# Second cross attention: value projections filled for four heads and two key tiles at a time, with three value buffers and half the DMA scratch of GpSimd

## The reference

```python
x = layernorm(x, gamma_media, beta_media)            # context, 1601 rows
latents = layernorm(latents, gamma_lat, beta_lat)    # the decoder's 512 rows
kv = concatenate((x, latents * kv_gate), axis=1)     # 2113 rows
q = (latents @ Wq).reshape(b, n, 8, 64)
k = (kv @ Wk).reshape(b, f + n, 8, 64)
v = (kv @ Wv).reshape(b, f + n, 8, 64)
sim = einsum('bqhd,bkhd->bhqk', q * SCALE, k)
sim = sim - max(sim, axis=-1)
sim = where(valid, sim, NEG_INF)
attn = softmax(sim, axis=-1)
out = einsum('bhqk,bkhd->bqhd', attn, v)
return out.reshape(b, n, 512) @ Wout
```

## Time and profile before

| | |
|---|---|
| median of three runs | 2273.76 us (2272.56 to 2274.42) |
| the profiled execution | 2277.54 us |
| its span, first to last instruction | 2275.8 us |
| busy TensorE matmul, weight load | 89 %, 62 % of the span |
| busy VectorE, ScalarE, GpSimd | 67 %, 51 %, 42 % |
| mean granted clock of TensorE | 0.952 |
| the slots 1 to 31 of the second cross attention | 943.8 to 1893.5 us of the span |

### The profile page before, as it was taken

One profiled execution on the slowest core, in us unless ns is written; L12 is line 12 of the kernel. 1 busy time (PEld: TensorE's weight loads), 2 busy tenths in 40 slices (PEclk: granted clock), 3 DMA queues, 4 the chain that ended last, 5 costly groups with the idle time before them and its releaser, 6 DMA issues. The chain is left out here.

```text
span 2275.8 us, 35924 instructions
## 1 busy us (share of the span) xinstructions
PE 2025.2 (89%) x12772; PEld 1411.3 (62%) x12772; DVE 1521.8 (67%) x2434; ACT 1161.3 (51%) x2234; POOL 954.1 (42%) x754
## 2 busy tenths in 40 slices
PE   7888868996989996899999999999999997699995
PEld 4555547994343544566666656565666664699995
DVE  5687864552887887688788768877787886322223
ACT  3332311102367456768766877677776773233333
POOL 2233232322221131166665656675666665222222
PEclk9999978998999997999999999999999998799998
DMA  4100016311000000100000000000000001631113
GB/s 157 39 25 20 25 62 261 130 35 63 0 0 0 1 29 22 46 1 1 30 1 1 10 19 12 1 11 1 1 1 1 10 1 42 237 112 38 38 33 121
DMA packets 36780, 93.32 MB, mean 41 GB/s; under 512 B 5479, under 2 KB 24443, under 8 KB 31998
## 3 DMA queue, kind: packets, MB, share of 16 engines
q1 hardware_dynamic: 30526, 74.72, 9.2%
q0 software_dynamic: 6080, 16.29, 2.1%
HBM read 76.56 MB, written 14.44 MB: 40 GB/s over the span
## 5 line engine op out<-in xcount | busy, mean ns | idle before, releaser
L2107 POOL TENSOR_TENSOR x_total<-x_total,x_pt 128x1024 f32<-128x1024 f32 x189 | 446.5, 2362 | 171.4 <-ACT x_pt L2193 153.8
L2215 ACT ACTIVATE x_pt<-PS,x_maskf 128x512 f32<-128x512 f32 x544 | 332.1, 689 | 166.6 <-PE PS L2529 162.0
L2314 DVE TENSOR_TENSOR PS<-x_pt,PS 128x512 f32<-128x512 f32 x480 | 333.4, 695 | 65.5 <-ACT x_pt L2215 27.5
L2332 DVE TENSOR_TENSOR x_pt<-x_pt,PS 128x1024 f32<-128x1024 f32 x320 | 320.4, 1052 | 0.7 <-PE PS L2547 0.7
L2529 PE MATMUL PS<-x_qs,x_ks 64*128 64x256 f32 x2176 | 282.0, 395 | 1.5 <-ACT x_pt L2215 1.5
L2506 PE MATMUL PS<-x_pt,x_vs 128*64 128x256 f32 x2108 | 264.0, 389 | 20.9 <-issue 12.1
L2193 ACT ACTIVATE x_pt<-x_pt 128x1536 f32<-128x1536 f32 (+1 forms) x160 | 266.5, 1667 | 13.9 <-DVE x_pt L2332 13.9
L1161 PEld LDWEIGHTS PS<-m_xT,m_own 128*128 128x128 f32 x1984 | 234.7, 195 | 10.2 <-DVE m_own L1241 7.2
L1161 PE MATMUL PS<-m_xT,m_own 128*128 128x128 f32 x1984 | 235.7, 278 | 5.9 <-DVE m_own L1241 5.9
L2529 PEld LDWEIGHTS PS<-x_qs,x_ks 64*128 64x128 f32 x2176 | 199.4, 188 | 65.1 <-issue 39.1
L2506 PEld LDWEIGHTS PS<-x_pt,x_vs 128*64 128x64 f32 x2108 | 142.6, 137 | 138.3 <-issue 68.8
(11 more groups left out here) (309 smaller groups left out, 2925.3 us busy)
## 6 DMA issues: line engine op xcount, KB each, us to landing
f_w<-in_L_ffn_w SPq DMA_DIRECT2D x32, 1024.0 KB
a_ctxT<-in_ctxT SPq DMA_DIRECT2D x8, 800.5 KB, 4.3
f_w<-ys SPq DMA_DIRECT2D x24, 256.0 KB, 5.5
l_w<-in_ctx SPq DMA_DIRECT2D x4, 1024.0 KB
l_w<-in_L_attn_w SPq DMA_DIRECT2D x6, 512.0 KB
a_xT<-in_xT SPq DMA_DIRECT2D x4, 512.0 KB, 5.8
X<-in_x SPq DMA_DIRECT2D x1, 2048.0 KB, 11.2
xr<-a_xn SPq DMA_DIRECT2D x16, 128.0 KB, 1.7
```

What stands on the lines that cost most here:

```text
L2107: ins = nc.gpsimd.tensor_tensor(total2[:], first, tile[:, 2 * k + 2:2 * k + 4, :], ALU.add)
L2215: nc.scalar.activation(pt[:, s % 2, t, :].rearrange("p (h n) -> p h n", h=2), PS[:, first:first + 2, half], ACT.Identity, bias=maskf[:, b ...
L2314: ins = nc.vector.tensor_tensor(acc, tile, acc, ALU.max)
L2332: nc.vector.tensor_tensor(p_, p_, PS[:, MB, None, :].to_broadcast([P, at.stop - at.start, SPAN]), ALU.subtract).then_inc(lowered, 1)
```

## The change

A V fill now covers two pairs (four heads, 256 columns) and two key tiles: `("V", b, n, c)` with n the group in its batch and c = 0 to 8, of which the last has one tile. The nine fills of a group are laid out by a table: the five places of the first unit's slot (c 0 to 4), gi 0 of the second (c 5), gi 0, 1 and 2 of the third (c 6, 7, 8), none in the fourth. At gi 0 of the second and third slot q or K leads, so V is a trail fill there. The even pair of a group uses buffer 0, the odd pair buffers 1 and 2 in turn. The reciprocal's tile `rb` moves into a part of a weight tile that is free by then, and the DMA scratch of GpSimd is set to 8192 bytes a partition.

```diff
-        vs = sb("vs", [P, 2, KT, 2 * HDX])
+        vs = sb("vs", [P, 3, KT, 2 * HDX])
...
-        rb = sb("rb", [P, QN])
+        rb = g["x_rb"]
...
+        VCHUNKS = -(-KT // 2)
+        VALUES_AT = {(0, 0): 0, (0, 1): 1, (0, 2): 2, (0, 3): 3, (0, 4): 4, (1, 0): 5, (2, 0): 6, (2, 1): 7, (2, 2): 8}
+        def value_tiles(c):
+            return range(2 * c, min(2 * c + 2, KT))
+        def value_chunk(gi):
+            return (EDGES[gi + 1] - 1) // 2
+        def value_buffers(n):
+            return (0, 1 + n % 2)
+        def value_buffer(b, p):
+            n = b * PAIRS_X // 2 + p // 2
+            return value_buffers(n)[p % 2]
...
-                    made.append(("V", b, p, gi))
...
+                if (i % 4, gi) in VALUES_AT:
+                    made.append(("V", b, i // 4, VALUES_AT[i % 4, gi]))
...
-                    ts = TILES[use[3]]
-                    ins = nc.scalar.copy(vs[:, use[2] % 2, ts.start:ts.stop, :],
-                                         src[:, 0:len(ts) * 2 * HDX].rearrange("p (t d) -> p t d", t=len(ts)))
+                    _, b, n, c = use
+                    ts = value_tiles(c)
+                    one, two = value_buffers(b * PAIRS_X // 2 + n)
+                    ins = nc.scalar.copy(vs[:, one:two + 1:two - one, ts.start:ts.stop, :].rearrange("p c t d -> p t c d"),
+                                         src[:, 0:len(ts) * 4 * HDX].rearrange("p (t c d) -> p t c d", t=len(ts), c=2))
...
-                    for i, t in enumerate(TILES[c]):
+                    for i, t in enumerate(value_tiles(c)):
                         for k in range(KD):
-                            mm = nc.tensor.matmul(out[:, i * P:(i + 1) * P], kvT[:, b % 2, k, t * P:(t + 1) * P],
-                                                  wv[:, k, p * P:(p + 1) * P], start=(k == 0), stop=(k == KD - 1))
+                            mm = nc.tensor.matmul(out[:, i * 2 * P:(i + 1) * 2 * P], kvT[:, b % 2, k, t * P:(t + 1) * P],
+                                                  wv[:, k, 2 * n * P:2 * (n + 1) * P], start=(k == 0), stop=(k == KD - 1))
...
-                        released(pe, ("V", b, p, gi))
+                        released(pe, ("V", b, p // 2, value_chunk(gi)))
...
-    nc = bacc.Bacc("TRN2", target_bir_lowering=False, num_devices=1)
+    nc = bacc.Bacc("TRN2", target_bir_lowering=False, num_devices=1, dynamic_dma_scratch_size=8192)
```

More of the change, by code:

```diff
@@ L1420, in first_context @@
     g["x_most"] = w[:, 1, at + PAIRS_X * D:at + PAIRS_X * D + 512]
+    g["x_rb"] = w[:, 1, at + PAIRS_X * D + 512:at + PAIRS_X * D + 512 + 256]
     g["x_loaded_first"] = ctx.enter_context(nc.semaphore("x_loaded_first"))
@@ L1928, in exists @@
             return 0 <= u < UNITS
+        VCHUNKS = -(-KT // 2)
+        VALUES_AT = {(0, 0): 0, (0, 1): 1, (0, 2): 2, (0, 3): 3, (0, 4): 4, (1, 0): 5, (2, 0): 6, (2, 1): 7, (2, 2): 8}
+        assert sorted(VALUES_AT.values()) == list(range(VCHUNKS))
+        def value_tiles(c):
[7 more added lines that the diff above has]
+            return value_buffers(n)[p % 2]
         CGROUPS = [("ctx", t, min(4, CT - t)) for t in range(0, CT, 4)] + [("lat", 0, J)]
@@ L2453, in fill @@
                 elif kind == "V":
-                    _, b, p, c = use
+                    _, b, n, c = use
                     pe.wait_ge(gated, b + 1)
-                    for i, t in enumerate(TILES[c]):
+                    for i, t in enumerate(value_tiles(c)):
                         for k in range(KD):
-                            mm = nc.tensor.matmul(out[:, i * P:(i + 1) * P], kvT[:, b % 2, k, t * P:(t + 1) * P],
-                                                  wv[:, k, p * P:(p + 1) * P], start=(k == 0), stop=(k == KD - 1))
+                            mm = nc.tensor.matmul(out[:, i * 2 * P:(i + 1) * 2 * P], kvT[:, b % 2, k, t * P:(t + 1) * P],
+                                                  wv[:, k, 2 * n * P:2 * (n + 1) * P], start=(k == 0), stop=(k == KD - 1))
                 elif kind == "O":
@@ L2506, in weigh @@
                                 mm = nc.tensor.matmul(PS[h * HDX:(h + 1) * HDX, AVB, 0:QN],
-                                                      vs[:, p % 2, t, h * HDX:(h + 1) * HDX],
+                                                      vs[:, value_buffer(b, p), t, h * HDX:(h + 1) * HDX],
                                                       pt[:, u % 2, t, h * QN:(h + 1) * QN],
@@ L2574, in _ @@
                 pe.wait_ge(exp_done, u * NG + gi + 1)
-                released(pe, ("V", b, p, gi))
+                released(pe, ("V", b, p // 2, value_chunk(gi)))
                 for t in TILES[gi]:
                     for h in range(2):
-                        nc.tensor.matmul(PS[h * HDX:(h + 1) * HDX, FINAL_AVB, 0:QN], vs[:, p % 2, t, h * HDX:(h + 1) * HDX],
+                        nc.tensor.matmul(PS[h * HDX:(h + 1) * HDX, FINAL_AVB, 0:QN],
+                                         vs[:, value_buffer(b, p), t, h * HDX:(h + 1) * HDX],
                                          pt[:, u % 2, t, h * QN:(h + 1) * QN], start=(t == 0), stop=False)
```

## The result

The changed kernel takes 2293.78 us (median of five runs, 2288.11 to 2296.03), the kernel before 2274.42 (five runs, 2272.56 to 2278.66). The ratio is 1.0074, with a 95 % interval from 1.0058 to 1.0089, so between 13 and 20 us more. I had forecast 2291.3, which is +17.5; the medians alone differ by 19.4, and the ratio is worth 16.8.

The account below looks back on a forecast made before the run. It took VectorE's closed loop as the bound, TensorE close behind. Terms +16.5 + 5.4 - 6.4 + 2 = +17.5 on 2273.8 gave 2291.3 us; own range 2285 to 2298, 8 in 10 within 2281 to 2300.

Parts of the forecast that it names:

- The bound: Attention stage: a plain slot lasts as long as VectorE's chain, with TensorE some 0.6 us ahead of it.
- The first rival: Whole stage: TensorE sets the pace throughout, so only its own sum counts, -5 us, 2269 us; chance 0.06.
- the second: V fills: wide matmuls cost 0.6 of two narrow ones, -12.6 us, 2261 us; chance 0.02.
- the third: Third slots give more back: O slots in full, 2 each in 6, 14, 22; +8 to +10, 2283 us; chance 0.12.
- The price of a fill: TensorE: a new fill of eight wide matmuls takes 1.83 us behind the transpositions, 1.93 as a lead fill.
- Second slots: Slots 1, 5, ... 29: c 5 between `turned` and the scores costs 5 x 1.74 and 3 x 2.6, together +16.5 us.
- First slots: Slots 0, 4, ... 28: longer lead fills cost four x 0.3 and four x 1.05 us, together +5.4.
- Third slots: Slots 2, 6, ... 30: TensorE relieved of 3.6 us each, of which the slots give back 6.4 in sum.
- The clock: TensorE idling 3.6 us ahead of `weigh` in slots 2, 6, 14, 22, 30 lowers its clock: +2 us, bounds 0 and 6.5.
- Memory and ScalarE: Other edits (ScalarE's moves, third value buffer, `rb`, halved DMA scratch): taken as 0, with 3 us as upper end for the scratch.

Follow-up runs that it names:

- e1: Changed kernel with c 5 taken out of the second slots; third slots carry c 5 to 8 at gi 0 to 3: 2279.88 us, ratio 1.0009.
- e7: Changed kernel with c 5 and c 6 both at gi 0 of the second slots, c 7 and 8 at gi 1 and 2 of the third: 2297.01 us.
- e3: Changed kernel with c 5 moved within the second slots from gi 0 to gi 2: 2290.95 us, ratio 1.0064.
- e4: Kernel before with the memory edits alone (third value buffer unused, reciprocal's tile moved, scratch 8192 bytes): 2277.37 us, ratio 0.9999.
- e12: Changed kernel with c 0-3 at gi 1-4 (first slots), c 4 at gi 4 (second), c 8, 5, 6, 7 at gi 0-3 (third): 2262.07 us, ratio 0.9934.
- e5: Changed kernel with no second-slot fill; third slots carry c 5 and 6 at gi 1 and 2, c 7 and 8 at gi 3: 2276.14 us.
- e6: Changed kernel with c 0-3 at gi 1-4 (first slots), none in second, c 4-5, 6, 7-8 at gi 1, 2, 3 (third): 2275.50 us.

## Why the prediction was right, point by point

**The bound.** The closed loop through VectorE, with TensorE close behind, was the right reading. e1 against the changed kernel shows that one fill's place carries the loss, e7 that it doubles, e3 that TensorE's chain has no room either. The first rival (TensorE paces all, 2269 us) and the second (cheap wide matmuls, 2261) are out. Of the third (3.6 us given back in each O slot, 2 in each of 6, 14 and 22) the part on 6, 14 and 22 came true and the part on the O slots did not; its sum, too, comes to +7 and not to the +8 to +10 written.

**The price of a fill.** Forecast 1.83 behind the transpositions and 1.93 as a lead; measured 1.82 and 1.92. Eight wide took 1.82 where sixteen narrow took 1.88, a ratio of 0.97. The spacing that the Trainium skill gives ("TensorE: Matmul & The Clock Gate", Back-to-back issue gap) would have made it about 0.6, by the prediction's estimate; for this float32 shape the measurement decides.

**Second slots: +18.9 for +16.5.** The five plain ones: 1.73 in slots 1 and 17 as forecast, 2.0 in 25 and 29 (0.3 of it is work of the first slot before that shows in the wait for `turned`), and 0.4 in slot 9, where the trace before had the clock fall of the earlier trace rows. The three with transpositions gave 2.8, 3.8 and 4.4 where I had 2.6 each; their wait at the first maximum is 4.16 as forecast (about 4.2). In slots 13 and 21, the two that gave more, the mean granted clock is 0.91 and 0.96 in the changed kernel's trace, and 0.95 and 1.00 in the trace before.

**First slots: +3.8 for +5.4.** Slot 0 gave 1.1, slot 24 nothing in itself and 0.3 in the next, slot 28 0.4 where I had put 1.05. Slots 12 and 20 (-0.6 and +3.0) are mixed with falls of the clock: slot 12 has 0.95 on the mean in the trace before and 1.00 after, slot 20 1.00 before and 0.91 after. Without slot 20 the eight would be at +0.9, so that the sum came near is luck.

**Third slots: -12.6 for -6.4.** This is the term that I mis-sized, and the traces show the greater part of why. For slots 6, 14 and 22 I took 0.4 each, reading TensorE as level at their end. They gave 2.25, 2.25 and 1.6. In the kernel before, slot 6, gi 3, TensorE and then VectorE:

```profile
1110.74 0.66 PE L2433 MATMUL PS<-ident,x_ln 128*128 128x128 f32 x4 [0.70 <-ACT x_vs L2165]
```

```profile
1113.23 2.30 DVE L2314 TENSOR_TENSOR PS<-x_pt,PS 128x512 f32<-128x512 f32 x3 [1.81 <-ACT x_pt L2215]
```

and in the kernel after, the same place:

```profile
1116.19 0.66 PE L2456 MATMUL PS<-ident,x_ln 128*128 128x128 f32 x4
```

```profile
1119.36 2.30 DVE L2337 TENSOR_TENSOR PS<-x_pt,PS 128x512 f32<-128x512 f32 x3 [0.19 <-ACT x_pt L2238]
```

The transposition N had to wait for the V fill's move, which stood behind an exponential; with no V fill at gi 3 nothing of the kind is left. My sum did not have this wait of VectorE. e1 puts a fill back at gi 3, and slot 6 gives only 0.5 again. The slots with output products gave 0.8, 2.1 and 1.9 (forecast 1.3, 1.3, 2.5). The rest is slot 2, which gave 1.7 for a forecast of 0.05: in the trace before its V fill at gi 0 ran at a granted clock of 0.69 (the window 970.0 to 975.5) and took 2.97 us in place of 1.88, and in the changed kernel's trace no such fall lies there. As far as the traces show, that is the clock and not the change's relief.

**The clock: +2.** Right in direction, wrong in size and place. I had TensorE idle some 3.6 us in five slots. It idles 5.9 in one piece at the end of slots 2 and 30, and at most 1.2 in 6, 14 and 22, whose relief shortened the slots. The 5.9 is the 3.6 on top of an idle time that I had missed: the trace before has 2.34 and 2.29 in the same two places. After both long ones the clock falls. TensorE at the start of slot 31 of the kernel after, and the window around it:

```profile
1875.51 3.68 PE L2529 MATMUL PS<-x_pt,x_vs 128*64 128x256 f32 x16 [5.89 <-ACT x_pt L2216]
```

```profile
1874.30:1881.10 6.80, 5.59 (x24) 3.46 (x26) 3.75 (x6) 0.50 (x1) 6.51 (x3) 0.50 0.00 0
```

and VectorE's product that frees the bank, which ends at 1875.40, later than the exponential that the row above names:

```profile
1874.98 0.42 DVE L2366 TENSOR_TENSOR x_o<-PS,l_w 128x256 f32<-128x256 f32 x1
```

Sixteen matmuls take 3.68 us in place of the 1.95 of the earlier trace rows, and slots 3 and 31 are 1.6 and 2.4 us longer. Together that is 4.0, twice the 2 forecast, which the other six fourth slots, 0.15 shorter each, bring to the 3.1 of the table. The falls in other slots, of which some came (13, 20, 21) and some went (2, 9, 12), are in the other terms and can't be told from the change there.

**Memory and ScalarE.** Nothing that e4 and e1 could tell from zero, as forecast. ScalarE's strided copy of 512 columns takes 589 ns on the mean, the plain one 586.

So the stage's sum was 13.1 for a forecast of 17.5 and the time came out at 2293.8 for 2291.3. The mis-sized third slots (I had counted 6 us too little given back) were partly made up by the second slots, by the longer falls of the clock and by 2.8 us outside the slots; that the total was so close is partly luck.

## What to carry to other kernels

Work that an engine issues between two halves of a hand-over (here: maximum turned, scores not yet there) is paid in full by the engine that waits, though the issuing engine does less in sum. So before an edit that moves work, look for the idle time that recurs once a cycle on the engine that seems to have room, see what stands in the other queue at that moment, and put the movable work at the place where the waiting engine has something long of its own to do (here gi 4 with its reciprocal, where e12 paid 1.0 us of a fill's 1.93 in a plain slot). Two fills that share one bank, or a fill that is read in its own place, cost the time until a third engine's queue reaches the move (0.42 to 2.18 us in these traces).

## What was not expected

A stretch of code that no edit touched ended between 922.3 (e12) and 930.0 us (e4) after the start in these traces, and the runs of the kernel before lay between 2272.6 and 2282.6 us; differences under 0.2 % are therefore read from the slots and not from the totals, and even there a fall of the clock can hide 1 to 3 us of a slot.

The clock fell to 1.2 GHz for about 6.8 us behind the idle times of 5.9 us in slots 2 and 30. But the length of the idle time alone doesn't decide. In the kernel before, 2.23 at the end of slot 8 was followed by a fall, and 2.34 and 2.29 at the ends of slots 2 and 30 by none (the next sixteen matmuls took 1.95 each time). At the end of slot 30 two versions idle equally long; TensorE in e5, then in e6:

```profile
1860.49 3.61 PE L2528 MATMUL PS<-x_pt,x_vs 128*64 128x256 f32 x16 [3.21 <-ACT x_pt L2215]
```

```profile
1865.54 1.95 PE L2528 MATMUL PS<-x_pt,x_vs 128*64 128x256 f32 x16 [3.21 <-ACT x_pt L2215]
```

What else decides it, these runs don't show.
